# Flat step lists for the filling and draining of a two-layer transformer's second attention

## The chip, the cores and the metric

The kernel runs on one core of a Trainium2 chip. Its time is the device time of one execution in microseconds (us). A core has five engines with queues of their own: TensorE (matmuls into PSUM; PE in the profile, its weight loads PEld), VectorE (DVE), ScalarE (ACT), GpSimd (POOL) and SyncE (SP), which here issues the transfers. Each runs its queue in order and waits on semaphores. PSUM has eight banks of 128 x 512 floats.

## What is computed

Two transformer layers with layer norm after each sublayer, on x of 2 x 512 x 256 in float32:

```python
x = layernorm(x + L0_attn(x))   # 16 heads of 16; relu(scores + 0.1), causal, divided by the row's sum
x = layernorm(x + L0_ffn(x))    # Hadamard transforms, silu(gate) * up, inner width 1024
x = layernorm(x + L1_attn(x))   # 32 query heads, 8 key heads of 64; rms norm, rope, window of 64, softmax
x = layernorm(x + L1_ffn(x))    # silu(gate) * up, inner width 1024
```

## The kernel before

Most products are made in three matmuls of high and low parts (`three`, L380): each operand is kept as a rounded high part, written by ScalarE, and a low part, the difference, written by VectorE (or by GpSimd for weights, L1200). So each result that feeds a further product costs a ScalarE and a VectorE instruction beside the matmuls.

Every engine has a program of its own that walks through the same list of steps and executes those that concern it. The first part, attention of layer 0, is a list for each engine (`TENSOR_FIRST` and so on). Behind it stands one common list, `LATER` (L140 to L179), of large steps:

- `ffn(layer, n)`, n from 0 to 15 (batch n // 8, block of 128 inner rows n % 8): the up of block n (12 matmuls of 512 columns), then the down of block n - 2 (12 of 256 columns). ScalarE makes silu and the high part, VectorE the product and the low part. The hidden rows have three buffers.
- `attn1(k)`, 22 passes for the 16 groups of layer 1's attention (batch k // 8, key head k % 8). A pass runs, in an order written out for each engine (`TENSOR_PASS` and the others, L46 to L54), the pieces of several groups: `proj1` of group k - 1 (four of 1), transposes of normed rows `turn1k`, `turn1q` and `scores1` of group k - 4, transposes of probabilities `turn_p` and `pv1` of group k - 5, `out1` of group k - 6. VectorE makes cosines, sums, `normed`, `maxima`, `probs`; ScalarE squares, copies, `exps`; GpSimd sines and inverse root mean squares.
- `ln(layer, b)`: addition to the rows, statistics, and (after GpSimd's inverse deviation) normalisation of all four row blocks of a batch, in one piece; `xt(layer, b)`: their transposes.
- `chunk(name, c)`: the split of a chunk of weights. SyncE loads chunks in the order of `CHUNKS` into three slots; each load waits for the split of the chunk three before.

`LATER` starts `attn1` 0, 1 and 2 behind `ffn(0, 13)`, `(0, 14)` and `(0, 15)`, then runs whole passes; `ffn(1, 0)` and `(1, 1)` stand behind passes 19 and 20, the other steps of the second network behind the last pass. `xt(3, 1)` stands behind `ffn(1, 2)`. `ln_last` (L994) takes the last layer norm by halves.

Results go to six PSUM banks in turn (`claim`, L367); banks 6 and 7 are the accumulators `y` of the downs and of `out1`. A claim waits until the bank's last user has read it. Buffers of layer 1 lie over those of layer 0: `roped`, `q_t`, `k_t`, `probs` over layer 0's network weights, `ug1` and `down1` over the weights `qkv`. `normed(0)` (L1093) therefore waits for the last down of layer 0.

## Time and profile before

| | us |
|---|---|
| median of three runs (lowest, highest) | 527.74 (526.45, 528.85) |
| the profiled execution | 527.04 |
| its span, first to last instruction | 524.4 |
| mean granted clock of TensorE | 0.979 |

The stages of the profiled execution: attention of layer 0 until about 100 us; layer 0's network from 100 to 180.8; layer 1's attention from 165 to 451.9, of which the six passes 7 to 12 take 234.24 to 325.04; the second network from 451.9 to 517.1; the last layer norm and the store until 524.4. Busy times are those of the hardware profiler; a matmul's time on the timeline overlaps with the next one's, so start-to-start differences give its rate. The number in brackets behind a timeline row is the idle time ahead of it and who ended it.

### The profile page before, as it was taken

To read this page: it belongs to the slowest core of one execution; us is meant where nothing else is said; L and a number is where in the kernel's file an instruction comes from. 1 tells how busy PE (TensorE), PEld (TensorE's weight loads), DVE (VectorE), ACT (ScalarE), POOL (GpSimd) and SP (SyncE) were. 2 spreads that over 40 slices of the span, in tenths; PEclk is the share of its full clock that TensorE was granted. 3 is DMA by queue.
4 is the path that set the end of the run, shared out by engine and by line. 5 is a ranking of instruction groups with operands and counts; after the bars stand their busy time and mean duration, and the time that the engine had idled before them with its cause. 6 is when DMAs were issued, how large, how long until landed. Compare 5 with 4: busy or idle time off the path is not lost.

```text
span 524.4 us, 10779 instructions
## 1 busy us (share of the span) xinstructions
PE 472.9 (90%) x3848; PEld 400.3 (76%) x3848; DVE 385.0 (73%) x675; ACT 335.9 (64%) x940; POOL 236.1 (45%) x167
## 2 busy tenths in 40 slices
PE   2899997999999975999999999988996988899994
PEld 2454654788889964899999999978896877788884
DVE  4455597778562689998898998889889974543534
ACT  3555555634643439888888989859888798332230
POOL 0377537221640756655566566545656523400001
PEclk9999998999999997999999999989999899999998
DMA  8500010033310000000000000001001222000101
GB/s 272 176 16 2 2 41 0 1 120 92 97 66 20 1 1 0 23 20 3 22 23 21 21 23 21 8 15 40 24 12 50 62 62 81 1 0 1 41 0 40
DMA packets 8611, 19.96 MB, mean 38 GB/s; under 512 B 1392, under 2 KB 2928, under 8 KB 8432
## 3 DMA queue, kind: packets, MB, share of 16 engines
q1 hardware_dynamic: 8560, 19.29, 11.9%
q8 instruction: 31, 0.51, 0.4%
q14 instruction: 20, 0.16, 0.1%
HBM read 18.23 MB, written 1.05 MB: 37 GB/s over the span
## 4 chain that ended last, share of the span: by engine, by line
PE 72%; DVE 11%; ACT 8%; issue 5%; POOL 1%; DMA 1%; DVEq 0%; POOLq 0%; ACTq 0%; SPq 0%
PE psum L383 16%; PE psum L385 15%; PE psum L384 15%; PE psum L614 5%; PE psum L430 4%; PE psum L602 4%; PE psum L592 4%; ACT probs L846 4%; PE psum L448 4%; PE psum L573 2%; DVE minus_max L1122 1%; PE psum L582 1%; DVE rope_cos_part L1078 1%; DMA raw_chunks<-in_w 1%; DVE out_t_low L897 1%
## 5 line engine op out<-in xcount | busy, mean ns | idle before, releaser
L846 ACT ACTIVATE probs<-psum,minus_max 128x128 f32<-128x128 f32 x256 | 92.6, 398 | 18.7 <-PE psum L592 10.4
L1240 POOL TENSOR_TENSOR rope_sin_part<-qkv_rows,sin_weighted 128x640 f32<-128x640 f32 x32 | 49.1, 1556 | 62.3 <-DVE rope_cos_part L1091 39.5
L1249 POOL TENSOR_TENSOR rms_inverse<-rms_inverse,minus_half 128x20 f32<-128x20 f32 x16 | 64.0, 3999 | 1.3
L846 ACT ACTIVATION_READ_ACCUMULATOR probs<-psum,minus_max 128x1 f32 x256 | 60.4, 236 | 0.0
L818 ACT CAST hidden_high<-hidden 128x512 fp32r<-128x512 f32 x32 | 19.8, 620 | 62.4 <-DVE hidden L1037 62.4
L1122 DVE TENSOR_REDUCE minus_max<-psum 128x4 f32<-128x512 f32 x64 | 42.4, 684 | 15.7 <-PE psum L592 14.3
L383 PE MATMUL psum<-x_t_high,ug_high 128*128 128x512 f32 x128 | 51.2, 400 | 0.0
L385 PE MATMUL psum<-x_t_high,ug_low 128*128 128x512 f32 x128 | 50.7, 396 | 0.0
L384 PE MATMUL psum<-x_t_low,ug_high 128*128 128x512 f32 x128 | 50.4, 394 | 0.0
L1116 DVE TENSOR_TENSOR probs<-probs,prob_inverse 128x512 f32<-128x512 f32 x64 | 47.6, 744 | 2.2
L383 PE MATMUL psum<-qkv_high,x_t_high 128*128 128x384 f32 x128 | 46.3, 362 | 0.0
L823 ACT COPY qkv_rows<-psum 128x384 f32<-128x384 f32 x64 | 32.4, 509 | 19.0 <-PE psum L385 19.0
L1200 POOL TENSOR_TENSOR wout_low<-raw_chunks,wout_high 128x512 fp32r<-128x512 f32 x16 | 20.8, 1301 | 52.2 <-ACT wout_high L751 52.2
L385 PE MATMUL psum<-qkv_high,x_t_low 128*128 128x384 f32 x128 | 43.6, 341 | 0.0
L384 PE MATMUL psum<-qkv_low,x_t_high 128*128 128x384 f32 x128 | 43.6, 341 | 0.0
L614 PE MATMUL psum<-probs_t,v_rows 128*64 128x128 f32 x512 | 35.7, 282 | 8.7 <-ACT probs_t L854 8.7
L936 DVE TENSOR_SCALAR weights_t<-psum 128x384 f32<-128x384 f32 (+1 forms) x48 | 26.6, 596 | 21.3 <-PE psum L430 21.3
L383 PE MATMUL psum<-wout_high,out_t_high 128*128 128x256 f32 x128 | 38.7, 302 | 2.5 <-DVE x_rows L962 2.5
L775 ACT ACTIVATE weights_t<-psum,bias_threshold 128x384 f32<-128x384 f32 (+1 forms) x48 | 27.0, 616 | 21.7 <-PE psum L430 21.7
L1207 POOL TENSOR_SCALAR_AFFINE_SELECT weights_t<-weights_t 128x512 f32<-128x512 f32 x32 | 21.8, 694 | 36.8 <-DVE weights_t L936 21.0
L1040 DVE TENSOR_TENSOR hidden_low<-hidden,hidden_high 128x512 fp32r<-128x512 f32 x32 | 22.2, 692 | 22.0 <-ACT hidden_high L818 22.0
L614 PEld LDWEIGHTS psum<-probs_t,v_rows 128*64 128x64 f32 x512 | 28.0, 138 | 13.1 <-issue 8.5
(146 smaller groups left out, 1403.4 us busy)
## 6 DMA issues: line engine op xcount, KB each, us to landing
raw_chunks<-in_ug SPq DMA_DIRECT2D x8, 512.0 KB, 3.9
raw_chunks<-in_wout SPq DMA_DIRECT2D x16, 256.0 KB, 2.8
raw_chunks<-in_qkv SPq DMA_DIRECT2D x8, 384.0 KB, 3.3
raw_chunks<-in_x SPq DMA_DIRECT2D x2, 512.0 KB, 4.5
raw_chunks<-in_w SPq DMA_DIRECT2D x2, 512.0 KB, 6.4
down_tree<-in_down SPq DMA_DIRECT2D x1, 1024.0 KB, 8.4
x_rows<-in_x_rows SPq DMA_DIRECT2D x2, 512.0 KB, 4.8
raw_chunks<-in_down SPq DMA_DIRECT2D x2, 512.0 KB, 3.4
```

The lines of the kernel that those rows point to most:

```text
L383: nc.tensor.matmul(o, ah_, bh_, start=first, stop=False, **kw)
L384: nc.tensor.matmul(o, ah_, bl_, start=False, stop=False, **kw)
L385: return nc.tensor.matmul(o, al_, bh_, start=False, stop=last, **kw)
L614: mm = nc.tensor.matmul(o[64 * h2:64 * h2 + 64, cols], v1[:, k % 5, 1 - q4 % 2, 2 * half_ + q4 // 2, :], prt[:, 2 * half_ + h2, cols], sta ...
L775: nc.scalar.activation(wt[:, hg % 2, h4, at:at + w], o[:, 0:w], ACT.Relu, bias=bias0[:]).then_inc(done, 1)
L823: nc.scalar.copy(qraw[:, k % 2, t, :], o[:, 0:GV]).then_inc(done, 1)
L846: e = nc.scalar.activation(pr[:, c, q, :], o[:, q * P:(q + 1) * P], ACT.Exp, bias=negm[:, c, q:q + 1], accum_out=psum1[:, c, q:q + 1])
L936: nc.vector.tensor_scalar(wt[:, hg % 2, h4, at:at + w], o[:, 0:w], -ATTN_THRESHOLD, 0.0, ALU.add, ALU.max).then_inc(done, 1)
L1116: nc.vector.tensor_tensor(pr[:, c], pr[:, c], pinv[:, c, :].rearrange("p (q a) -> p q a", a=1).to_broadcast([P, 4, P]), ALU.mult).then_inc ...
L1122: nc.vector.tensor_reduce(negm[:, c, :], o.rearrange("p (q w) -> p q w", q=4), AX.X, ALU.max, negate=True).then_inc(mx_done[c], 1)
L1240: last = nc.gpsimd.tensor_tensor(ov[:, :, :, z, :], rv[:, :, :, 1 - z, :], sv[:, :, :, z, :], ALU.mult)
L1249: nc.gpsimd.tensor_tensor(r, r, half[:], ALU.pow).then_inc(rr_done, 1)
```

## The change

`LATER` is replaced by five parts. `BETWEEN` holds ups 4 to 9 and downs 2 to 7 of layer 0 with the chunks of `qkv` 0 to 5 and `ln(1, 0)`. Then a list for each engine (`TENSOR_FILL` and so on) holds the rest of layer 0's network, passes 0 to 6 in single pieces, `ln(1, 1)` in pieces and both transposes. `STEADY_STEPS` are passes 7 to 12 as before. A second list for each engine (`TENSOR_DRAIN` and so on) holds passes 13 to 21 in single pieces, ups 0 to 7 and downs 0 to 5 of layer 1, `ln(2, 0)` and `ln(2, 1)` in pieces. `LAST` holds the rest, the last three downs by halves of the rows. `ffn` is split into `up` and `down`. The high and low parts of weights lie side by side for each chunk, so that layer 1's buffers can take their places piece by piece, with waits for the pieces' last readers; layer 1's hidden rows have six buffers. The pieces of a pass inside the four lists may stand in another order than in `TENSOR_PASS` and the others.

```diff
-EARLY_AT = [NI + 5, NI + 6, NI + 7]
+STEADY = (7, 13)
 SLOTS = 3
-FLAG = 2
+HIDDEN_SLOTS = [3, 6]
-FFN1_CHUNKS = [("ug1", c) for c in range(4)] + [("down1", c) for c in range(2)]
+FFN1_CHUNKS = [("ug1", 0), ("ug1", 1), ("down1", 0), ("ug1", 2), ("ug1", 3), ("down1", 1)]
+FFN1_OVER = [(8 * i + 7) // 6 for i in range(len(FFN1_CHUNKS))]
+TENSOR_FILL = [("up", 0, 10), ("down", 0, 8), ("down", 0, 9), ("up", 0, 11), ("xt", 2, 0), ("down", 0, 10),
+    ("up", 0, 12), ("up", 0, 13), ("proj1", 0, 0), ("proj1", 0, 1), ("down", 0, 11), ("proj1", 0, 2), ("proj1", 0, 3),
+    ("up", 0, 14), ("down", 0, 12), ("up", 0, 15), ("down", 0, 13), ("proj1", 1, 2), ("down", 0, 14), ("down", 0, 15),
+    ("proj1", 1, 0), ("proj1", 1, 1), ("proj1", 1, 3), ("proj1", 2, 2), ("proj1", 2, 3), ("proj1", 2, 0),
+    ("proj1", 2, 1), ("xt", 2, 1), ("turn1q", 0, 1), ("turn1k", 0), ("turn1q", 0, 0), ("proj1", 3, 1),
+    ("scores1", 0, 0), ("proj1", 3, 0), ("proj1", 3, 2), ("proj1", 3, 3), ("scores1", 0, 1), ("turn1q", 1, 0),
...
+VECTOR_FILL = [("up", 0, 10), ("up", 0, 11), ("up", 0, 12), ("xt", 2, 0), ("up", 0, 13), ("up", 0, 14),
+    ("values1", 0), ("up", 0, 15), ("square_sums", 0), ("cosines", 0), ("ln_add", 1, 1, 0), ("ln_stats", 1, 1, 0),
+    ("ln_add", 1, 1, 1), ("ln_stats", 1, 1, 1), ("rope_sums", 0), ("ln_norm", 1, 1, 0), ("ln_norm", 1, 1, 1),
+    ("square_sums", 1), ("values1", 1), ("normed", 0), ("values1", 2), ("cosines", 1), ("xt", 2, 1),
...
+TENSOR_DRAIN = [("out1", 7, 0), ("proj1", 12, 1), ("turn1q", 9, 0), ("turn1k", 9), ("turn_p", 8, 1), ("proj1", 12, 0),
...
+    ("out1", 13, 0), ("turn_p", 14, 2), ("turn1q", 15, 1), ("turn_p", 14, 0), ("turn_p", 14, 1), ("scores1", 15, 0),
+    ("turn_p", 14, 3), ("scores1", 15, 1), ("pv1", 14, 0), ("out1", 13, 1), ("pv1", 14, 1), ("up", 1, 0),
+    ("out1", 14, 0), ("turn_p", 15, 0), ("turn_p", 15, 1), ("turn_p", 15, 2), ("turn_p", 15, 3), ("out1", 14, 1),
+    ("pv1", 15, 0), ("pv1", 15, 1), ("up", 1, 1), ("out1", 15, 0), ("out1", 15, 1), ("up", 1, 2), ("down", 1, 0),
+    ("up", 1, 3), ("up", 1, 4), ("down", 1, 1), ("up", 1, 5), ("up", 1, 6), ("down", 1, 2), ("down", 1, 3),
+    ("down", 1, 4), ("xt", 3, 1), ("up", 1, 7), ("down", 1, 5)]
+VECTOR_DRAIN = [("values1", 11), ("rope_sums", 10), ("probs", 8, 3), ("maxima", 9, 0), ("maxima", 9, 1),
+    ("square_sums", 11), ("normed", 10), ("pv1", 8, 0), ("maxima", 9, 3), ("maxima", 9, 2), ("probs", 9, 0),
+    ("probs", 9, 1), ("ln_add", 2, 0, 0), ("pv1", 8, 1), ("ln_stats", 2, 0, 0), ("ln_add", 2, 0, 1), ("cosines", 11),
+    ("probs", 9, 2), ("ln_stats", 2, 0, 1), ("probs", 9, 3), ("values1", 12), ("ln_norm", 2, 0, 0),
...
+def last_steps():
+
+    s = []
+    for n in range(8, B * NI):
+        s.append(("up", 1, n))
+        if n != 12:
+            s.append(("down", 1, n - 2 if n < 12 else n - 3))
         if n == NI + 1:
             s.append(("ln", 3, 0))
-    s.append(("ln_last",))
+    for half_ in range(2):
+        s += [("down", 1, n, half_) for n in range(B * NI - 3, B * NI)]
+        s += [("ln_add", 3, 1, half_), ("ln_stats", 3, 1, half_), ("ln_half", half_)]
+    s += [("ln_norm", 3, 1, half_) for half_ in range(2)]
     return s
...
         with ExitStack() as s:
             qn = place(s, "roped", [TT, GN], F32)
+            qt1 = place(s, "q_t", [2, NQ, 2, WIN], F32)
+            place(s, "until_down0", [512])
+            kt1 = place(s, "k_t", [2, T], F32)
             wol = place(s, "wout_low", [2, 2, C], F32R)
-            qt1 = place(s, "q_t", [2, NQ, 2, WIN], F32)
-            kt1 = place(s, "k_t", [2, T], F32)
             pr = place(s, "probs", [4, 4, P], F32)
...
+                if (name, c) in FFN1_CHUNKS:
+                    filled(act, ("proj1", KV + FFN1_OVER[FFN1_CHUNKS.index((name, c))], TT - 1))
...
                 o, done = take(act, ("turn1k", k))
+                if k == 0:
+                    filled(act, ("ffn", 0, NI + 6, 1))
...
                     filled(act, ("turn1p", k - 1, c))
+                else:
+                    filled(act, ("ffn", 0, B * NI - 1, 0))
...
                     filled(act, ("pv1", k - 1, c // 2))
+                else:
+                    filled(act, ("y", 1, B - 1, 1))
...
             def wout(k):
+                if k == 0:
+                    filled(act, ("y", 1, B - 1, 1))
...
                 if k == 0:
-                    filled(dve, ("y", 1, B - 1, 1))
+                    filled(dve, ("ffn", 0, NI + 3, 0))
```

## Rows read from the trace of the kernel before

**Rows 1.** The page, busy time of each engine with its share of the span.
```profile
PE 472.9 (90%) x3848; PEld 400.3 (76%) x3848; DVE 385.0 (73%) x675; ACT 335.9 (64%) x940; POOL 236.1 (45%) x167
```

**Rows 2.** Busy us by stage: stretch, length, PE, PEld, DVE, ACT, POOL, clock, DMA.
```profile
143.10:180.00 36.90, 36.62 (x217) 33.13 (x216) 19.66 (x40) 16.68 (x27) 12.76 (x9) 1.00 0.11 33
180.00:234.24 54.24, 44.04 (x377) 39.77 (x375) 49.48 (x82) 39.35 (x133) 33.56 (x21) 0.94 0.02 6
234.24:325.04 90.80, 90.80 (x866) 83.28 (x864) 82.68 (x133) 81.03 (x282) 54.90 (x31) 1.00 0.06 19
...
340.00:417.00 77.00, 68.87 (x656) 62.58 (x652) 72.01 (x115) 60.76 (x206) 44.72 (x25) 0.96 0.12 36
417.00:451.90 34.90, 29.40 (x273) 26.27 (x272) 21.00 (x36) 29.06 (x94) 11.37 (x7) 1.00 0.17 54
451.90:517.10 65.20, 63.63 (x370) 55.37 (x368) 29.49 (x58) 17.92 (x30) 4.68 (x5) 1.00 0.03 9
```

**Rows 3.** Timeline of TensorE: start, us, instruction, idle time ahead and its end.
```profile
201.90 0.90 PE L573 MATMUL psum<-identity,roped 128*128 128x128 f32 x3 [6.09 <-DVE roped L1107]
...
344.24 0.38 PE L383 MATMUL psum<-wout_high,out_t_high 128*128 128x256 f32 x1 [2.53 <-DVE x_rows L962]
...
406.48 0.33 PE L614 MATMUL psum<-probs_t,v_rows 128*64 128x128 f32 x2 [2.67 <-ACT probs_t L854]
...
457.59 0.33 PE L487 MATMUL psum<-identity,x_rows 128*128 128x128 f32 x1 [1.32 <-DVE x_rows L978]
```

**Rows 4.** Busy us in two short stretches of the drain, columns as above.
```profile
345.10:348.50 3.40, 3.40 (x16) 3.30 (x16) 1.78 (x8) 0.13 (x1) 1.27 (x2) 0.53 0.00 0
407.00:410.40 3.40, 3.40 (x24) 3.07 (x21) 3.33 (x7) 3.40 (x18) 3.23 (x3) 0.54 0.48 143
```

**Rows 5.** VectorE's waits from 174.5 to 234.3: total us, times, longest.
```profile
DVE x_rows L978 <- POOL ln_rstd L1220: 1.5, 1, 1.5
...
DVE square_sums L1084 <- POOL rms_inverse L1249: 0.9, 1, 0.9
```

**Rows 6.** Timeline of TensorE behind the last down of layer 0: first and last of 24.
```profile
180.80 0.34 PE L383 MATMUL psum<-qkv_high,x_t_high 128*128 128x384 f32 x1
...
184.86 0.34 PE L385 MATMUL psum<-qkv_high,x_t_low 128*128 128x384 f32 x1
```

**Rows 7.** Timelines of VectorE and TensorE at the end of pass 6.
```profile
229.95 1.22 DVE L1107 TENSOR_TENSOR roped<-rope_cos_part,rms_inverse 128x1024 f32<-128x1024 f32 x1
...
234.24 0.33 PE L573 MATMUL psum<-identity,roped 128*128 128x128 f32 x1
```

**Rows 8.** Drain: timelines, VectorE's waits of 325 to 452, groups of the page.
```profile
348.46 1.39 DVE L978 TENSOR_SCALAR x_rows<-x_rows,ln_mean_var,ln_rstd 128x256 f32<-128x256 f32 x4 [1.55 <-POOL ln_rstd L1220]
...
DVE minus_max L1122 <- PE psum L592: 6.8, 5, 2.6
...
396.37 2.50 POOL L1200 TENSOR_TENSOR ug_low<-raw_chunks,ug_high 128x1024 fp32r<-128x1024 f32 x1
396.59 2.44 DVE L1067 COPY v_rows<-qkv_rows 128x256 f32<-128x256 f32 x1
412.49 2.06 DVE L1116 TENSOR_TENSOR probs<-probs,prob_inverse 128x512 f32<-128x512 f32 x1
420.80 1.70 DVE L1116 TENSOR_TENSOR probs<-probs,prob_inverse 128x512 f32<-128x512 f32 x1
...
L1116 DVE TENSOR_TENSOR probs<-probs,prob_inverse 128x512 f32<-128x512 f32 x64 | 47.6, 744 | 2.2
L1200 POOL TENSOR_TENSOR wout_low<-raw_chunks,wout_high 128x512 fp32r<-128x512 f32 x16 | 20.8, 1301 | 52.2 <-ACT wout_high L751 52.2
```

**Rows 9.** Timelines of TensorE and VectorE at the end.
```profile
516.78 0.28 PE L385 MATMUL psum<-down_high,hidden_low 128*128 128x256 f32 x1
...
516.38 0.69 DVE L962 TENSOR_TENSOR x_rows<-psum,x_rows 128x512 f32<-128x512 f32 x1 [1.53 <-PE psum L385]
...
518.06 0.66 DVE L962 TENSOR_TENSOR x_rows<-psum,x_rows 128x512 f32<-128x512 f32 x1
```

More of the change, by code:

```diff
@@ L387, in _, with first @@
             acc = {}
+            begun = set()
+            def first(step, k):
+                new = (step, k) not in begun
+                begun.add((step, k))
+                return new
             def x_ready(layer, b):
@@ new lines, in up @@
+            def up(layer, n):
+                b, i = divmod(n, NI)
+                if i == 0:
+                    x_ready(1 + 2 * layer, b)
+                if layer == 0:
+                    emptied(pe, *[("prep_ug", i // 2, m) for m in range(KB)])
+                else:
+                    chunk_wait(pe, ("ug1", i // 2))
+                wh, wl = [up_weights(layer, i // 2, z) for z in range(2)]
+                for u in (1, 0):
+                    o, done = claim(("ffn", layer, n, u))
+                    for kb in range(KB):
+                        at = kb * 512 + (i % 2) * 256 + u * P
+                        mm = three(o, (wh[:, at:at + P], wl[:, at:at + P]), (xh[:, b, kb, :], xl[:, b, kb, :]),
+                                   kb == 0, kb == KB - 1)
+                    mm.then_inc(done, 1)
@@ L959, in ln_add @@
             def ln_add(layer, b, half_):
+                if layer == 0 and half_ == 0:
+                    dve.wait_ge(rows_in[b], 16)
                 o, done = take(dve, ("y", layer, b, half_))
```

297 lines of the change are left out of this document (157 added, 140 removed), and 41 rows, old and new, of tables (SCALAR_DRAIN, SCALAR_FILL, SCALAR_FIRST, TENSOR_DRAIN).

## The prediction

> **What bounds the kernel now.** I read the busy shares first. TensorE is busy for 472.9 of 524.4 us, and no other engine is above 385.0 [rows 1]. That share is an average, so I cut the span into stages [rows 2]. In the steady passes of layer 1's attention (234.24 to 325.04, six passes of 15.13 us) TensorE is busy for all of 90.80 us, VectorE for 82.7 and ScalarE for 81.0: TensorE sets the pace and VectorE has 1.35 us to spare in a pass. The losses lie at both sides of that stretch. While the pipeline fills (143.1 to 234.24), TensorE stands for 0.3 + 10.2 us. While it drains (340 to 451.9) it stands for 8.1 + 5.5 us, and in the second feed-forward network for 1.6 us, of which 1.3 are one stall [rows 3].
>
> Next I asked who is full where TensorE stands. From 180 to 234.24 VectorE is busy for 49.5 of 54.2 us, and from 340 to 417 for 72.0 of 77.0 us [rows 2]. So there TensorE waits for a vector engine that has hardly any room: 91% and 94% busy against 91% in the steady stretch. From 417 to 451.9 nobody is full (TensorE 29.4, ScalarE 29.1, VectorE 21.0 of 34.9 us): that is a chain of short steps. In two of the stalls the granted clock fell from 2.4 to 1.2 GHz afterwards while TensorE had work: both stretches of 3.4 us show a mean near one half [rows 4], so each cost about 1.7 us.
>
> This gives floors. If all idle time of TensorE and both slow stretches went, the fill could give 10.5 us and the drain 13.6 + 3.4 = 17.0 us. VectorE's floor is lower: it has the same work as before, so by it the fill gives only its own idle time there, and the drain up to 417 only 5.0 us.
>
> **The change, part by part.** The sets of instructions are the same in both kernels; nothing is computed more or less. What changes is their order in each engine's queue.
>
> *Fill.* Before, the queues run whole feed-forward steps (an up and the down two behind), then whole passes. The new lists interleave: the first projections stand ahead of ups 14 and 15, passes are mixed with the last downs, and layer norm comes in pieces. The new places of the buffers allow it: the normed rows no longer wait for the last down of layer 0 but for up 11. This wait doesn't bind before, since the last down ends at 180.80 [rows 6], ahead of the first normed rows; I cost it at nothing. Three of the eight projection steps that stood ahead of the last down now stand behind it. One projection step is (184.86 + 0.18 - 180.80) / 4 = 1.06 us [rows 6], so the last down ends 3.2 us earlier, at 177.6.
>
> What does VectorE make of that? Its waits in the fill are, first, 1.5 us for the layer norm's inverse deviation and 0.9 us for the inverse root mean square [rows 5]. Layer norm in pieces puts the sum of the rotated rows between statistics and normalisation, so the first wait goes; the earlier projections take the second. That is 2.4 us, and it is what VectorE gains by the end of the fill. TensorE can gain more, as far as VectorE's results are ready early. The last normed rows of the fill end at 229.95 + 1.22 = 231.17, and their first transpose starts at 234.24 [rows 7]: 3.1 us to spare. So TensorE can gain up to 2.4 + 3.1 = 5.5 us, and the steady passes, in which VectorE has 1.35 us to spare each, let it make up the lost lead. The stall of 6.1 us ahead of the second pass's transposes [rows 3] shrinks, since now four projections and both score steps stand between the first and second normed rows. Ahead of the first normed rows a stall grows: with three projections moved behind the last down TensorE is out of work at 186, while VectorE has the layer norm and two sums to do first, until 189 or 190. I count 4.5 us for the fill, nearer to 5.5 than to 2.4 because TensorE, not VectorE, sets the passes that follow; both ends stay in the range, and at the low end a gain of only 1 us, should the new stall cost more.
>
> *Added waits.* Layer 1's buffers now overlap layer 0's in smaller pieces, so ScalarE gets waits of its own: the first keys' copy for up 14, the first exponentials for up 15, the first copy of probabilities and the first output weights for the last down, each chunk of the second network's weights for one projection group of the second half. Behind each the whole of ScalarE's queue waits. By TensorE's order the awaited step ends before the producer of the waiting one begins (the last down at 177.6, the first probabilities after 199; the projections four and more passes ahead of the chunks), so they cost nothing; if TensorE's order didn't cover them, each would cost at most one up, 2.9 us.
>
> *Drain.* Layer norm of the first half of the batch was queued whole at the end of pass 13. TensorE stood 2.53 us before it could start the next accumulation [rows 3], then had a slow stretch [rows 4], and VectorE itself stood 1.55 us for GpSimd [rows 8]. Now its first addition stands ahead of the last product of pass 8 and the cosines, probabilities and values of the next passes stand between its pieces. This removes 1.55 us from VectorE; of the other 3.5 us that it idles up to 417, mostly waits for scores (6.8 us in all, with those behind 417) [rows 8], I take 2. Together 3.5 us. From 417 on the step chain decides: scores of the last pass, maxima, exponentials, transposes, product, output. The new lists turn the keys and queries of passes 14 and 15 ahead of earlier output products, so that the last scores come sooner, and put output products and the first up of layer 1's network where TensorE waits for exponentials. The last pass's own chain through ScalarE and VectorE stays: its exponentials, its four copies, its two products. Of the 5.5 us that TensorE idles there [rows 2] I take 3, and so the last output product ends at 451.9 - 3.5 - 3 = 445.4. The first stall of the drain goes; the second [rows 3] shrinks. Below these values nothing but 1.5 us for the layer norm is sure; above them stands 13 us, if VectorE's 5.0 us and most of what TensorE loses behind 417 and to the clock come back. Those are the ends for the drain.
>
> *Start of the second network.* The transposes of the second half wait 1.32 us for layer norm [rows 3], after one up and one down. The new list has five ups and five downs in between, with six instead of three buffers for the hidden rows: 1.3 us off, and nothing is late next, since the weights of the fourth chunk are loaded and split long before the up that reads them. The queue of loads keeps its order except that down chunk 0 moves ahead of the third up chunk; the whole core moves 36 to 54 GB/s there [rows 2], so nothing for it.
>
> *End.* The last accumulation ends at 517.1 on TensorE [rows 9]. Its addition starts only at 518.06, because VectorE is still at the first half, which began at 516.38. With the last three downs by halves the first half is complete three half-steps earlier, and the second addition starts with the last matmul: 518.06 - 517.1 = 1.0 us. The final normalisation's wait for GpSimd stays. The same number of matmuls runs, so the halving costs nothing on TensorE.
>
> Sum: 4.5 + 6.5 + 1.3 + 1.0 = 13.3 us. The profiled execution took 527.04 us (span 524.4), which gives 513.7; the median of the three runs is 0.7 us higher, so 514.4 us.
>
> **A rule weighed.** VectorE's copy of values at 396.59 took 2.44 us, where GpSimd ran a subtraction of 2.50 us from 396.37, and two products of probabilities took 2.06 and 1.70 us where their mean is 0.744 us [rows 8]. So a collision can hold VectorE for nearly the whole of GpSimd's instruction; these three cost about 2 + 1.3 + 1.0 = 4.3 us, and they are in the sum as they stand. The Trainium skill (SBUF — State Buffer, Who interferes with whom) says that VectorE instructions with two SBUF inputs, and some copies, contend with GpSimd instructions that read SBUF, and that the loser blocks for the whole instruction. By that rule, the trace agrees. It speaks against a list that fills VectorE's gaps, since a fuller VectorE meets more of GpSimd's instructions; by the rows alone the sum stays at 13.3 us, by the rule at its worst it is that of the last rival.
>
> **The rivals.** *VectorE is the bound (15 in 100).* Then TensorE gets nothing beyond VectorE's own idle time in the fill and little in the chain: 2.4 + 3.5 + 1.3 + 0.5 = 7.7, so 520.0. For it: 91 and 94% busy where it matters. Against it: the lead of 3.1 us, and steady passes in which it recovers.
>
> *Near TensorE's floor (10 in 100).* Fill 8, drain 13, 1.3 and 1.0: 23.3 us, so 504.4. For it: no engine's work forbids it behind 417. Against it: VectorE's floor before that.
>
> *No change (7 in 100).* The stalls only move: the new wait at 186 and others like it in the drain take the place of 6.1, 2.5 and 2.7 us; only start and end give, 2.3 us, so 525.4.
>
> *Slower by collisions (6 in 100).* In the packed drain each of GpSimd's two-input subtractions hits VectorE: eight of 1.3 us for the output weights and five of 2.5 us for the second network's chunks [rows 8], 22.9 us in all, where 4.3 us are lost already. The other 18.6 us against the 13.3 won give 5.3 us more than before: 533.0. It decides from 13.3 us of added blocking. Against it: the same subtractions beside a VectorE that is 94% busy cost only 4.3 us now.
>
> **How the numbers follow.** The forecast has 62 in 100; most of its spread is 509 to 519. The range of 506 to 522 takes in the first rival; it leaves out the floor, no change and the slower case, and they hold 23 in 100, less the part of the floor case that reaches above 506, so about 20. A measurement of this kernel can tell 0.5% from no change (525.1 to 530.4). Faster by more: 62 + 15 + 10 = 87; same 7; slower 6.
>
> **What would show it.** Steps right: no TensorE wait for the normed rows near 200 above 2 us, one of 2 to 4 us near 186 to 190; steady passes of 15.13 us that begin about 4.5 us earlier; no wait for the layer norm's addition at pass 14; the last output product ending 10 to 12 us earlier; the transposes of the second half without a wait; 6.2 instead of 7.3 us from the last matmul to the end. It is wrong if VectorE's busy time in the drain grows by over 5 us (collisions), if steady passes lengthen, or if the granted clock falls in new places while TensorE has work.

## The result and the profile after

The changed kernel took 519.73 us (median of four runs, 518.33 to 521.9) against 527.1 us for the kernel before (526.25 to 528.85): ratio 0.986, 95% interval 0.9815 to 0.9899. Timed again later in five rounds it took 520.17 us against 528.34 us, ratio 0.9845 (0.982 to 0.987). The forecast was 514.4 us with a range of 506 to 522. So the sign and the range held. Of the forecast gain of 13.3 us, 7.4 to 8.2 us came.

The profiled execution took 520.81 us with a span of 519.1 us. Busy times hardly differ from [rows 1]: no work went away, it stands closer together.

```profile
PE 475.5 (92%) x3848; PEld 399.3 (77%) x3848; DVE 384.5 (74%) x675; ACT 335.8 (65%) x940; POOL 240.5 (46%) x167
```

The stages again, cut where they now end: fill, steady passes, drain in two parts, second network, tail (stretch, length, busy us of PE, PEld, DVE, ACT, POOL, granted clock, DMA). They answer [rows 2].

```profile
181.00:235.00 54.00, 47.04 (x379) 42.40 (x379) 48.39 (x81) 42.15 (x139) 35.52 (x20) 0.94 0.02 6
235.00:326.00 91.00, 91.00 (x872) 83.37 (x866) 82.90 (x136) 81.11 (x282) 55.69 (x32) 1.00 0.07 19
...
341.00:417.00 76.00, 67.17 (x651) 59.74 (x648) 71.56 (x116) 62.44 (x215) 47.38 (x27) 1.00 0.14 42
417.00:449.10 32.10, 30.86 (x287) 26.71 (x286) 19.51 (x38) 27.34 (x88) 7.62 (x4) 1.00 0.14 45
449.10:512.70 63.60, 63.38 (x369) 55.28 (x367) 32.22 (x62) 18.50 (x31) 7.69 (x7) 1.00 0.03 9
512.70:519.10 6.40, 0.00 (x1) 0.00 (x0) 3.05 (x9) 0.00 (x0) 1.73 (x3) 0.69 0.24 82
```

Behind 417 TensorE stands for 1.2 us where it stood for 5.5. Ahead of it, it still stands for 8.8 of 76 us, and VectorE is as full as it was. Next, TensorE's timeline, where it still waits (start, us, instruction, idle time ahead and its end). The stalls of 6.09, 2.53 and 1.32 us of [rows 3] are gone, and others stand elsewhere.

```profile
191.25 1.12 PE L696 MATMUL psum<-identity,roped 128*128 128x128 f32 x4 [2.92 <-DVE roped L1238]
...
201.72 0.39 PE L705 MATMUL psum<-window_mask,eye_twice 64*128 64x512 bf16 x2 [1.04 <-ACT probs L977]
204.26 1.04 PE L696 MATMUL psum<-identity,roped 128*128 128x128 f32 x5 [1.25 <-ACT probs L977]
...
406.17 0.65 PE L688 MATMUL psum<-identity,roped 128*128 128x128 f32 x4 [0.96 <-DVE roped L1238]
407.68 0.63 PE L696 MATMUL psum<-identity,roped 128*128 128x128 f32 x4 [0.85 <-DVE out_t_low L1033]
413.25 0.39 PE L705 MATMUL psum<-window_mask,eye_twice 64*128 64x512 bf16 x2 [2.20 <-issue]
```

To compare many kernels I cut TensorE's timeline at four events that all of them have: A is the end of the last product with the Hadamard matrix (it prepares layer 0's last chunk of up weights, 1.6 us behind the second down), B the end of group 10's second projection (it lies in pass 11, one of the steady passes), C the end of the last output product, D the last matmul. A to B is what the expectations below call the part from the second neuron's product to the start of pass 10. Where they and I speak of a piece "of pass k", such as the scores of pass 14, the piece of group k is meant. "Half speed" is the time in that part during which the granted clock was 0.5 (1.2 GHz).

| kernel | median us | A | A to B (half speed) | B to C (half speed) | C to D | D to span's end |
|---|---|---|---|---|---|---|
| before | 527.1 to 528.3 | 116.39 | 183.91 (6.8) | 151.75 (3.4 + 3.4) | 65.02 | 7.3 |
| changed | 519.73 | 117.75 | 183.57 (3.4 + 3.4) | 147.85 (0) | 63.54 | 6.4 |
| again | 520.17 | 116.52 | 182.50 (0) | 147.76 (0) | 63.54 | 6.4 |
| fill_old | 520.39 | 116.74 | 183.90 (6.8) | 149.31 (3.4) | 63.54 | 6.4 |
| drain_old | 525.76 | 118.65 | 182.55 (3.4) | 152.80 (3 x 3.4) | 65.02 | 6.4 |
| last_whole | 521.65 | 117.40 | 183.71 (3.4 + 3.4) | 147.81 (0) | 63.54 | 7.3 |
| no_low | 518.74 | 116.69 | 184.55 (6.8) | 145.92 (0) | 63.54 | 6.4 |
| fill2 | 519.63 | 117.15 | 182.10 (6.8) | 149.26 (3.4) | 63.54 | 6.3 |
| warm | 521.17 | 116.69 | 184.88 (3.4) | 149.22 (3.4) | 63.54 | 6.4 |
| drain_old_warm | 524.87 | 116.73 | 183.84 (3.4) | 151.75 (3.4) | 65.01 | 6.4 |
| ln_pool | 522.73 | 116.42 | 184.63 (6.8) | 149.63 (3.4) | 63.54 | 6.4 |
| late_ug | 517.65 | 117.21 | 183.56 (3.4 + 3.4) | 146.51 (0) | 63.54 | 6.4 |
| best | 520.29 | 116.81 | 184.82 (6.8) | 146.88 (0) | 63.54 | 6.4 |
| fill3 | 523.04 | 116.97 | 187.63 (6.8 + 6.8) | 147.78 (3.4) | 63.55 | 6.4 |

The parts up to A hold the same work in all of them: A differs with a half-speed stretch of 3.4 or 6.8 us near 86 us. Two executions of one kernel differ by up to 3.6 us, and the time goes with the clock: the changed kernel's spans of 516.6 and 516.9 us had mean granted clocks of 0.989 and 0.990, those of 519.1 and 520.2 us 0.983. So the parts say more than a single total. The kernel before, timed beside each group of variants, had medians of 527.0 to 528.3 us, so between groups a difference of medians of about 1 us says little by itself.

From before to changed the parts add up: 0.3 to 1.4 us in A to B, 3.9 to 4.0 in B to C, 1.5 in C to D, 0.9 behind D, and 0.6 outside the span (see below), 7.2 to 8.4 us in all.

### The profile page after: what moved, and what is told of

Its sections match the earlier page's. It is cut to its first block, busy times and chain, and to the rows that moved or that the text cites. A ratio compares the mean times of both kernels' runs of the same rounds, so it can differ in the third digit from the quotient of the medians.

```text
span 519.1 us, 10798 instructions
## 1 busy us (share of the span) xinstructions
PE 475.5 (92%) x3848; PEld 399.3 (77%) x3848; DVE 384.5 (74%) x675; ACT 335.8 (65%) x940; POOL 240.5 (46%) x167
## 3 DMA queue, kind: packets, MB, share of 16 engines
HBM read 18.23 MB, written 1.05 MB: 37 GB/s over the span
## 4 chain that ended last, share of the span: by engine, by line
PE 77%; DVE 11%; ACT 5%; issue 4%; DMA 1%; POOL 0%; DVEq 0%; POOLq 0%; SPq 0%; ACTq 0%
PE psum L499 17%; PE psum L501 16%; PE psum L500 15%; PE psum L553 5%; PE psum L725 4%; PE psum L715 4%; PE psum L737 4%; PE psum L571 4%; PE psum L696 3%; ACT probs L977 3%; DVE minus_max L1253 2%; PE psum L705 2%; DVE roped L1238 1%; DVE square_sums L1215 1%; DMA raw_chunks<-in_w 1%
## 5 line engine op out<-in xcount | busy, mean ns | idle before, releaser
L1372 POOL TENSOR_TENSOR rope_sin_part<-qkv_rows,sin_weighted 128x640 f32<-128x640 f32 x32 | 51.2, 1623 | 48.6 <-DVE rope_cos_part L1222 42.3
L499 PE MATMUL psum<-x_t_high,ug_high_low 128*128 128x512 f32 x128 | 51.1, 399 | 0.0
L501 PE MATMUL psum<-x_t_high,ug_high_low 128*128 128x512 f32 x128 | 50.7, 396 | 0.0
L500 PE MATMUL psum<-x_t_low,ug_high_low 128*128 128x512 f32 x128 | 50.5, 395 | 0.0
L499 PE MATMUL psum<-qkv_high_low,x_t_high 128*128 128x384 f32 x128 | 47.1, 368 | 3.1 <-ACT qkv_rows L950 1.7
L500 PE MATMUL psum<-qkv_high_low,x_t_high 128*128 128x384 f32 x128 | 43.5, 340 | 0.0
L501 PE MATMUL psum<-qkv_high_low,x_t_low 128*128 128x384 f32 x128 | 43.4, 339 | 0.0
L987 ACT COPY probs_t<-psum 128x512 f32<-128x512 f32 x64 | 37.4, 626 | 0.5 <-PE psum L725 0.3
L725 PE MATMUL psum<-identity,probs 128*128 128x128 f32 x256 | 36.2, 275 | 1.4 <-ACT probs L977 1.2
L499 PE MATMUL psum<-down_high_low,hidden_high 128*128 128x256 f32 x128 | 36.4, 284 | 0.5 <-issue 0.5
```

The costliest lines, as they stand in the source:

```text
L499: nc.tensor.matmul(o, ah_, bh_, start=first, stop=False, **kw)
L500: nc.tensor.matmul(o, ah_, bl_, start=False, stop=False, **kw)
L501: return nc.tensor.matmul(o, al_, bh_, start=False, stop=last, **kw)
L725: mm = nc.tensor.transpose(o[:, q * P:(q + 1) * P], pr[:, c, q, :], ident[:])
L987: nc.scalar.copy(prt[:, c, :], o).then_inc(done, 1)
L1372: last = nc.gpsimd.tensor_tensor(ov[:, :, :, z, :], rv[:, :, :, 1 - z, :], sv[:, :, :, z, :], ALU.mult)
```

## The experiments

**Once more, unaltered.**

> The changed kernel itself once more, unaltered, beside the three that follow and timed in the same rounds as they are: 519.7 us by its first four runs (518.3 to 521.9), and with it the yardstick for the others. Nothing else is asked of it than how far its half-speed stretches move from one execution to the next: spans of 516.6 to 520.2 went with mean granted clocks of 0.990 to 0.983.

Its part A to B is 1.1 us shorter than in the first profile of the same kernel and holds no half-speed stretch; B to C agrees within 0.1 us. So the gain of 3.9 to 4.0 us in the drain repeats, and by these two the fill's is between 0.3 and 1.4 us.

**The fill's lists undone.** TENSOR_FILL and its three siblings hold the order of before:

```
...
+TENSOR_FILL = SCALAR_FILL = VECTOR_FILL = GPSIMD_FILL = fill_old()
```

> The changed kernel with layer 1's passes 0 to 6 and the rest of layer 0's network put back into the pass-by-pass order of before; buffers, the drain and the split tail stay as changed. Theory (the profile of the changed kernel gained only 0.3 us in the fill against its own offset, because VectorE's two named waits only moved): 519.5 to 521, that is 0 to 1 us above the changed kernel, and pass 7 starts about 234.7 us after the same half-speed stretches. Rival A (the prediction's sum: the lists of the fill are worth 4.5 us and the one profiled run hid it behind two extra half-speed stretches): 524, 4.5 us above the changed kernel. Rival B (the new order of the fill costs time): 517 to 519.

Measured: 520.39 us (520.08 to 521.61), 0.2 to 0.7 us above the changed kernel, as the theory has it. Rival A falls, and so does rival B. A to B is as before to 0.01 us, stall of 6.09 us included. Over the seven kernels that have the new fill unaltered (changed, again, drain_old, last_whole, no_low, drain_old_warm, late_ug), A to B is 182.50 to 184.55, mean 183.47: the lists of the fill are worth 0.4 us, which that spread of 2 us hardly tells from nothing, though layer 0's last down ends 2.3 us earlier behind A (62.3 us against 64.6).

**The drain's lists undone.**

```
...
+TENSOR_DRAIN = SCALAR_DRAIN = VECTOR_DRAIN = GPSIMD_DRAIN = drain_old()
```

> The changed kernel with layer 1's passes 13 to 21 and the first six neurons' steps of the second network put back into the order of before; the fill and the split tail stay as changed. Theory (the drain's lists gained 3.9 us and the stall before the second network 1.5): 524.5 to 525.5, that is 5 to 5.5 us above the changed kernel, and the stalls of 2.5 and 2.7 us near 344 and 406 us, each followed by a half-speed stretch, come back. Rival A (most of the 3.9 us was the two half-speed stretches that happened to be missing in the profiled run): only 1.5 to 3 us above. Rival B (the prediction's sum): 7.8 us above, 527.5.

Measured: 525.76 us (524.9 to 527.14), ratio to before 0.997 (0.995 to 0.998). That is 5.6 to 6.0 us above the changed kernel, just over the theory's 5 to 5.5 and far from rival A's 1.5 to 3 and rival B's 7.8: the theory holds in kind. The 1.48 us between C and D come back, and the profile shows three stalls, each followed by a half-speed stretch. First TensorE's timeline, then busy times of the three stretches, whose last figures but two are the granted clock:

```profile
345.22 0.39 PE L525 MATMUL psum<-wout_high,out_t_high 128*128 128x256 f32 x1 [2.50 <-DVE x_rows L1127]
...
407.27 1.11 PE L763 MATMUL psum<-probs_t,v_rows 128*64 128x128 f32 x16 [2.63 <-ACT probs_t L1013]
...
422.01 1.97 PE L763 MATMUL psum<-probs_t,v_rows 128*64 128x128 f32 x16 [2.38 <-ACT probs_t L1013]
```

```profile
347.00:350.20 3.20, 3.20 (x13) 3.10 (x13) 1.61 (x7) 1.25 (x3) 1.27 (x2) 0.50 0.00 0
408.30:411.60 3.30, 3.30 (x18) 3.29 (x17) 3.23 (x6) 3.30 (x16) 3.22 (x2) 0.50 0.49 160
422.00:425.30 3.30, 3.29 (x23) 2.97 (x24) 3.23 (x6) 2.56 (x14) 0.79 (x1) 0.50 0.36 97
```

**The stalls filled with work.** In that kernel, two of the three stalls get products whose result is overwritten:

```
                 o, done = claim(("pv1", k, half_))
+                for _ in range({(12, 1): 11, (13, 1): 10}.get((k, half_), 0)):
+                    nc.tensor.matmul(o, eye2[:], wmask[:, 0, :], start=True, stop=True)
```

> The kernel with the drain's old order (525.76 us), with 11 and 10 extra 512-column products, overwritten right behind, in the banks of the products of probabilities and values of passes 12 and 13, ahead of TensorE's waits for the transposed probabilities (stalls of 2.6 and 2.4 us at 407.3 and 422.0 us, each followed by a half-speed stretch). Theory (part of what the old order costs is not the stall but the half clock behind it): two stretches of 3.4 us go, and 2.5 to 3.4 us with them: 522.4 to 523.3. Rival (the stalls themselves are the cost, the slow stretches lie beside waits for VectorE): within 0.7 us of 525.8.

Measured: 524.87 us (523.77 to 526.98), 0.9 us less. Neither holds. The two half-speed stretches are gone, as the theory said, and the clock is 1.00 from 400 to 452:

```profile
346.00:349.30 3.30, 3.30 (x14) 3.20 (x13) 1.68 (x7) 0.80 (x2) 1.27 (x2) 0.50 0.00 0
400.00:452.00 52.00, 47.10 (x446) 39.65 (x442) 37.94 (x57) 41.07 (x137) 22.06 (x13) 1.00 0.18 57
```

But B to C falls only from 152.80 to 151.75: two stretches cost 1.05 us, not 3.4. The extra products didn't overrun the stalls: 0.23 and 0.37 us of them are left. In the old order TensorE waits again soon after a stretch, and that wait takes up most of what the half clock cost. At the full clock TensorE meets a wait here that the kernel without the extra products doesn't have:

```profile
412.75 0.63 PE L751 MATMUL psum<-identity,probs 128*128 128x128 f32 x4 [1.09 <-DVE out_t_low L1061]
```

In the new order, where it waits less behind 413, one such stretch costs more: 149.2 to 149.6 us with it (fill_old, fill2, warm, ln_pool) against 147.8 without (changed, again, last_whole), 1.4 to 1.8 us. All seven have the stall of 2.2 us, so it alone doesn't decide whether the stretch comes.

**The last downs whole again.**

```
-        s += [("down", 1, n, half_) for n in range(B * NI - 3, B * NI)]
+    s += [("down", 1, n) for n in range(B * NI - 3, B * NI)]   # once, ahead of both halves
```

> The changed kernel with the last three second projections of the network done as whole 512-column products again instead of by halves; all else as changed. Theory (the first half's addition and transfer now lie beside the second half's products): 520.5 to 520.9, 0.8 to 1.1 us above the changed kernel, and the time from the last product to the span's end is back from 6.4 to 7.3 us. Rival (the six half-width products cost as much as the hidden addition gives back, each half paying its own start): the same time within 0.3 us.

Measured: 521.65 us (521.03 to 522.14), 1.5 to 1.9 us above the changed kernel, 7.3 us from the last matmul to the end. C to D is 63.54 in both: the halving costs TensorE nothing. (The products have 256 columns in both kernels, since the halves are of the rows: the expectation's "512-column" and "half-width" products are a slip.) The parts give 0.9 us for the tail, as the theory says; the median lies 0.8 us above the theory's range, which is within the scatter. VectorE's timeline of this kernel (last matmul until 512.45) and of the changed one (until 512.70) shows the mechanism, the answer to [rows 9]: the addition of the first half has moved beside TensorE's last products.

```profile
511.77 0.69 DVE L1101 TENSOR_TENSOR x_rows<-psum,x_rows 128x512 f32<-128x512 f32 x1 [2.97 <-PE psum L501]
...
513.45 0.66 DVE L1101 TENSOR_TENSOR x_rows<-psum,x_rows 128x512 f32<-128x512 f32 x1
```

```profile
510.58 0.69 DVE L1101 TENSOR_TENSOR x_rows<-psum,x_rows 128x512 f32<-128x512 f32 x1 [1.53 <-PE psum L501]
...
512.74 0.69 DVE L1101 TENSOR_TENSOR x_rows<-psum,x_rows 128x512 f32<-128x512 f32 x1 [0.39 <-PE psum L501]
```

**GpSimd's subtractions in the drain left out.**

```
+                if name in ("ug1", "down1"):
+                    nc.gpsimd.memset(dst.bitcast(F32), 0.0).then_inc(ch_lo["pool"], 1)
+                    return
```

> The changed kernel with GpSimd's subtractions for the low parts of the second network's weights left out (a fill with zeros stands in their place, so that network lacks its low products' values but still runs all its products). It asks what GpSimd's two-input operations cost VectorE in the drain. Theory 1 (VectorE's stretched operations beside them, such as the 2.67 us product at 409.87 us, set the drain's end): 516.5 to 518, 2 to 3 us under the changed kernel, and the stall of 2.2 us at 411 us goes. Theory 2 (their cost lies beside TensorE's work, the gaps have other causes): within 0.7 us of the changed kernel, though VectorE's mean duration of the same operations falls.

Measured: 518.74 us (516.42 to 519.19), 1.0 to 1.4 us under the changed kernel; B to C falls by 1.9 us, and the stall of 2.20 us is gone. The median gained less than theory 1's 2 to 3 us and more than theory 2's 0.7 us; the part gained nearly what theory 1 asks, at no stretch of half speed in either, so here a collision does set the time. In the changed kernel it reads so, on VectorE and GpSimd:

```profile
409.87 2.67 DVE L1247 TENSOR_TENSOR probs<-probs,prob_inverse 128x512 f32<-128x512 f32 x1
412.46 0.68 DVE L1033 TENSOR_TENSOR out_t_low<-psum,out_t_high 128x512 fp32r<-128x512 f32 x1
...
409.48 2.52 POOL L1332 TENSOR_TENSOR ug_high_low<-raw_chunks,ug_high_low 128x1024 fp32r<-128x1024 f32 x1
```

The product of probabilities ends half a microsecond behind GpSimd's subtraction, and out_t_low behind it empties the bank that the scores of pass 14 wait for, the stall of 2.20 us.

**The one subtraction moved away.** Nothing is left out here; ScalarE's and GpSimd's part of one chunk go some 13 us later, from 407.9 and 409.5 to 421.3 and 422.6 us. (Not shown here: the chunk's load moves one place back in the queue of loads, and ScalarE's part of the next chunk moves behind five of its copies.)

```
-    ("exps", 13, 3), ("chunk", ("ug1", 1)), ("turn1q", 14, 1),          # ScalarE
+    ("exps", 14, 3), ("chunk", ("ug1", 1)), ("turn1k", 15),
-    ("chunk", ("ug1", 1)), ("wout", 13), ("chunk", ("down1", 0)),       # GpSimd
+    ("wout", 13), ("chunk", ("ug1", 1)), ("chunk", ("down1", 0)),
```

> The changed kernel with one preparation of the second network's weights moved back: ScalarE's rounded part from 407.9 us to about 424, GpSimd's subtraction from 409.5 us, where VectorE's multiplication of probabilities beside it took 2.67 us in place of 0.69, to about 425, where VectorE has slack. Theory (this one collision makes the stall of 2.2 us at 411 us that every kernel with the new drain shows, and in half of their runs a half-speed stretch behind it): the stall falls under 0.7 us, the drain from 147.8 to 146 us, the median from 520 to 517 to 518.3. Rival (the collision only moves to the new place): stall gone, but the drain within 0.5 us of 147.8.

Measured: 517.65 us (517.13 to 519.06), ratio to before 0.982 (0.980 to 0.984), the fastest of all. The theory holds: stall 0.22 us, B to C 146.51, no half-speed stretch. VectorE's same two instructions, GpSimd's moved one, and TensorE:

```profile
409.30 0.69 DVE L1247 TENSOR_TENSOR probs<-probs,prob_inverse 128x512 f32<-128x512 f32 x1
409.91 0.68 DVE L1033 TENSOR_TENSOR out_t_low<-psum,out_t_high 128x512 fp32r<-128x512 f32 x1
...
422.58 2.74 POOL L1332 TENSOR_TENSOR ug_high_low<-raw_chunks,ug_high_low 128x1024 fp32r<-128x1024 f32 x1 [9.46 <-ACT ug_high_low L877]
...
410.69 0.39 PE L705 MATMUL psum<-window_mask,eye_twice 64*128 64x512 bf16 x2 [0.22 <-issue]
```

Of the 2.0 us won at that stall 0.7 us are lost again behind it. So the drain gives 1.3 us. The medians differ by 2.1 to 2.5 us, but the kernel before didn't hold still between the groups either: by the ratios to it (0.9822 against 0.9845 and 0.9857, with intervals that overlap) the gain is 1.2 to 1.8 us, which agrees better with the part.

**Normed rows of pass 0 put forward.**

```
-    ("values1", 0), ("up", 0, 15), ("square_sums", 0), ...                # VectorE
+    ("values1", 0), ("square_sums", 0), ("up", 0, 15), ...
-    ("rope_sums", 0), ("ln_norm", 1, 1, 0), ("ln_norm", 1, 1, 1), ("square_sums", 1), ("values1", 1), ("normed", 0),
+    ("rope_sums", 0), ("normed", 0), ("ln_norm", 1, 1, 0), ("ln_norm", 1, 1, 1), ("square_sums", 1), ("values1", 1),
+    # TensorE and ScalarE: turn1q(0, 1), turn1k(0), turn1q(0, 0) ahead of xt(2, 1)
```

> The changed kernel with a few steps of the fill moved: VectorE sums the squares of pass 0 before the last hidden product of the network and multiplies pass 0's normed rows before it normalizes the layer norm's rows; TensorE, and ScalarE's copies with it, does the three turns of pass 0 before the transposes of the second sequence's rows. Theory (the fill gained nothing because VectorE's list puts pass 0's normed rows, which TensorE waits 2.9 us for at 188.3 us, behind a layer norm that itself waits 1.3 us for GpSimd): that stall goes to under 1 us and pass 7 starts 2 to 3 us earlier: 517 us. Rival (VectorE, busy 49.7 of 55.3 us there, is the bound of the fill, so that whatever is put forward is paid back by a later step): stall gone, but pass 7 starts within 0.7 us of where it did: 519 to 520.

Measured: 519.63 us (519.05 to 520.55), 0.1 to 0.5 us less. The stall of 2.9 us is gone, but TensorE's timeline shows it again, larger, at the scores of pass 0:

```profile
200.25 0.61 PE L705 MATMUL psum<-window_mask,eye_twice 64*128 64x512 bf16 x2 [5.58 <-ACT probs L977]
```

So something behind is full, as the rival says. Which engine, the next run asks.

**The layer norm's products on GpSimd.** Besides fill2's order:

```
+            # GpSimd, behind its inverse deviation; VectorE's ln_norm(1, 1) returns at once
+            for t in range(TT):
+                last = nc.gpsimd.tensor_scalar(xn[:, at, :], xn[:, at, :], mv[:, t, 0:1], rstd[:, t:t + 1],
+                                               ALU.subtract, ALU.mult)
```

> The kernel with the moved steps of the fill, and besides them the four normalizations of the second sequence's rows (1.39 us of VectorE, and the 1.33 us that it waited for GpSimd ahead of them) done by GpSimd itself, which stood idle for 2.98 us behind its inverses; what is computed is the same. Theory (VectorE's list is the bound of the fill): VectorE has 2.7 us less between the network's last products and pass 7, so the part from the second neurons' product to the start of pass 10 falls from 182.1 to 184.6 us (its half-speed stretches move it) to 180 to 181.5, and the median from 519.6 to 520.2 to 517.5 or below. Rival (TensorE's own work, or GpSimd's later inverses, bound the fill): the part stays at 182 or more and the median over 519.

Measured: 522.73 us (522.08 to 523.59), 2.6 to 3.0 us more than the changed kernel and 3.1 us more than fill2, its base. The theory falls. VectorE got its room and nobody gained. The tightest stretch of the fill, 186 to 205 us, as busy times in before, changed, fill2 and ln_pool:

```profile
186.00:205.00 19.00, 11.76 (x87) 10.65 (x88) 17.15 (x33) 11.02 (x40) 13.16 (x7) 0.83 0.00 0
```

```profile
186.00:205.00 19.00, 13.26 (x94) 11.86 (x93) 17.96 (x29) 11.74 (x37) 16.05 (x8) 0.90 0.00 0
```

```profile
186.00:205.00 19.00, 13.20 (x100) 12.21 (x99) 16.13 (x29) 12.29 (x39) 15.46 (x8) 0.82 0.00 0
```

```profile
186.00:205.00 19.00, 10.86 (x83) 9.67 (x82) 13.19 (x20) 10.02 (x29) 18.66 (x11) 0.83 0.00 0
```

In the last, VectorE falls to 13.2 and GpSimd rises to 18.7 of 19 us. So GpSimd, whose load the prediction never counted in the fill, has no room for this work: its inverse roots and sine products of passes 1 and 2 stand back to back behind it. The run moved the bound rather than finding it, since ln_pool's four products took 4.91 us on GpSimd, where VectorE needs 1.39:

```profile
184.53 4.91 POOL L1360 TENSOR_SCALAR x_rows<-x_rows,ln_mean_var,ln_rstd 128x256 f32<-128x256 f32 x4
189.52 0.66 POOL L1389 TENSOR_SCALAR rms_inverse<-square_sums 128x20 f32<-128x20 f32 x1
```

**Both together.**

> Both edits together: GpSimd normalizes the second sequence's rows with the fill's moved steps, and the one preparation is moved back. If each does what its theory says and they are independent: 1.5 to 2.5 us and 1.7 to 2.5 us under the changed kernel's 520.2: 515.5 to 517. If either is bound elsewhere: the better of the two alone, 517.5 to 518.5.

Measured: 520.29 us (520.17 to 520.75). The gain of the one and the loss of the other add up by the parts (184.82 and 146.88), so neither of the two outcomes came; ln_pool's theory fell in the same group of runs.

**Extra work in the fill's stalls.**

```
             def turn1q(k, hp):
-                pe.wait_ge(qn_done, k + 1)
                 o, done = claim(("turn1q", k, hp))
+                if (k, hp) in ((0, 1), (1, 0)):
+                    keep_busy(o, 12 if k == 0 else 5)
+                pe.wait_ge(qn_done, k + 1)
```

> The changed kernel with 12 and 5 extra 512-column products of the mask, overwritten right behind, in the banks of pass 0's and pass 1's first turned queries, put ahead of TensorE's wait for the normed rows (stalls of 2.9 and 1.2 us): what is computed is unchanged, TensorE only isn't idle there. Theory (the two half-speed stretches of the fill, which began at 190.9 and 204.5 us behind these stalls, follow from the idle time): they go, and 1 to 3 us with them: 517 to 518.5. Rival (the stretches come whatever TensorE does, or VectorE's pace hides them): 519.5 to 520.5, with the stretches still there or pass 7 starting as before.

Measured: 521.17 us (519.55 to 523.23), 1.0 to 1.4 us more. No stretch began near 190, but in "again" none did without the extra products either, so this says nothing on that stall. The other came, at 202.5, and the five extra products at 203.11 ran in it and took 2.32 us where they were meant to take half, so that the turns behind them started 2.0 us later behind A than in "again". Neither outcome came, and the run's six times fall in two groups, 519.6 to 519.9 us, as the changed kernel, and 522.4 to 523.2. It tells only that filling a stall can cost more than the stall.

**GpSimd's sine products first.** Base is late_ug:

```
-    ("rms_inverses", 1), ("sines", 1), ("rms_inverses", 2),             # GpSimd
+    ("sines", 1), ("rms_inverses", 1), ("rms_inverses", 2),
-    ("cosines", 1), ("xt", 2, 1), ("square_sums", 2), ("rope_sums", 1), ("maxima", 0, 0), ("normed", 1), ("maxima", 0, 1),
+    ("cosines", 1), ("maxima", 0, 0), ("maxima", 0, 1), ("square_sums", 2), ("rope_sums", 1), ("normed", 1),
+    # xt(2, 1) behind scores1(0, 1) on TensorE, behind exps(0, 1) on ScalarE, behind cosines(2) on VectorE
```

> The kernel with the one weight preparation moved back (517.65 us) and, in the fill, another order: GpSimd does pass 1's sine products before its inverse roots (at 185.2 us, where it stood idle for 3 us, in place of 191.9 us), VectorE takes the first two maxima of pass 0 before the squares of pass 2, the normed rows of pass 0 come first as in the kernel with the moved steps, and the second sequence's transposes come behind the scores of pass 0. Nothing is left out. Theory (GpSimd's order is what the fill waits for: ScalarE's copy of pass 3's first rows stands behind pass 1's sine products, which end at 195.0 us, and the exponentials, the banks and the stall of 5.6 us at 194.7 us stand behind that copy): that stall goes to under 2 us, the part from the second neuron's product to the start of pass 10 falls from 182.1 to 184.6 us to 178 to 181, and the median to 514 to 516. Rival A (VectorE's busy time, 49.7 of 55.3 us, is the bound whatever stands ahead): the part stays at 182 or more, the median within 0.7 us of 517.65. Rival B (the stall comes back at pass 1 or 2, since the inverse roots are later by 3 us): the same result as A, with a new stall of 2 us or more before pass 1's turns or pass 2's scores.

Measured: 523.04 us (521.91 to 524.45), 5.4 us above its base. The theory falls; what came is rival B and more. The stall of 5.6 us shrank only to 3.8 us, and two new ones of 2.2 us stand before the keys of pass 1 and the projections of pass 4, with two half-speed stretches of 6.8 us. One reason is plain in the rows of VectorE and GpSimd:

```profile
185.13 3.86 DVE L1120 TENSOR_SCALAR x_rows<-x_rows,ln_mean_var,ln_rstd 128x256 f32<-128x256 f32 x4
...
184.96 3.24 POOL L1372 TENSOR_TENSOR rope_sin_part<-qkv_rows,sin_weighted 128x640 f32<-128x640 f32 x2
```

VectorE's normalization took 3.86 us in place of 1.39: the sine products that I put into GpSimd's idle time fell on it, and what follows on VectorE came 2.5 us later behind A than in fill2. The run therefore doesn't settle whether GpSimd's order alone could win.

## Why the prediction was right or wrong

**Fill (4.5 us forecast, 0.4 measured): wrong.** The last down of layer 0 was to end 3.2 us earlier; behind A it ends 2.3 us earlier, since a new wait of 0.66 us stands before the first projection. The stall near 186 to 190 came as forecast (2.92 us), and so did the end of the 6.09 us one. The step that failed is "that is 2.4 us, and it is what VectorE gains". VectorE's waits between 174.5 and 235.3 us in the changed kernel, against [rows 5]:

```profile
DVE minus_max L1253 <- PE psum L715: 1.6, 3, 0.6
DVE x_rows L1120 <- POOL ln_rstd L1353: 1.3, 1, 1.3
...
DVE prob_inverse L1246 <- ACT probs L977: 1.2, 1, 1.2
```

The inverse root mean square's wait went; the layer norm's stayed. The statistics were ready at 182.97, GpSimd was at pass 0's inverse until 183.35, and then its small addition took 1.12 us. It took 0.23 us before. What held it is the very step that the new list puts between statistics and normalisation, VectorE's sum of the rotated rows. VectorE first, then GpSimd, all of the changed kernel:

```profile
182.89 1.46 DVE L1222 TENSOR_TENSOR rope_cos_part<-rope_cos_part,rope_sin_part 128x1280 f32<-128x1280 f32 x1
...
179.81 3.54 POOL L1381 TENSOR_TENSOR rms_inverse<-rms_inverse,minus_half 128x20 f32<-128x20 f32 x1
183.31 1.12 POOL L1352 TENSOR_SCALAR ln_var_eps<-ln_mean_var 128x4 f32<-128x4 f32 x1
184.52 1.05 POOL L1353 TENSOR_TENSOR ln_rstd<-ln_var_eps,minus_half 128x4 f32<-128x4 f32 x1
```

And GpSimd in the kernel before:

```profile
191.74 0.23 POOL L1219 TENSOR_SCALAR ln_var_eps<-ln_mean_var 128x4 f32<-128x4 f32 x1 [1.53 <-DVE ln_mean_var L971]
```

The addition took 1.12 or 1.38 us in all twelve profiles with the new order of these steps, and 0.23 us in before and fill_old, where no VectorE instruction stands beside it. So 0.9 of the 1.33 us are a collision that the new order made. Other waits replaced what went: VectorE is idle for 6.6 us from 174.5 to 235.3, where it was idle for 5.3 us from 174.5 to 234.3. In the 19 us from 186 VectorE is 95% busy in the changed kernel and GpSimd 84%. The other 2.1 us of the forecast, VectorE's lead at the end of pass 6, could not be used: TensorE has no wait above 0.7 us from 205 on, so its own work sets pass 7 from there, and it entered that stretch no earlier. In kind, the first rival, "VectorE is the bound", was nearer for the fill than the forecast; ln_pool shows that GpSimd is close to full there as well. Which of the two sets the fill, and what it would give with both engines' orders matched, is open: fill2, ln_pool and fill3 don't settle it.

**Added waits (costed at nothing): no sign against it, but not tested.** In ScalarE's timeline of the fill its waits stand before copies of projections, turned queries and keys, squares and scores, and none before the first probabilities' copy or the first output weights. They were not taken out one by one.

**Drain (6.5 us forecast, 3.9 to 4.0 measured, less with a half-speed stretch): half right.** From B to the scores of pass 14 it gained 1.1 us, where 3.5 were forecast; from there to the last output product 2.8, where 3 were forecast. The chain of short steps went as reasoned. VectorE's wait for the layer norm fell from 1.55 [rows 8] to 0.2 us, but the stalls around 350 to 411 us are many small ones, and the largest, 2.20 us, is a collision that I had named as a rival and priced only as a whole. The step that failed is "together 3.5 us": VectorE is idle for 4.4 of 76 us up to 417, where it was idle for 5.0 of 77 (the prediction's end at 445.4 us also leaves out the fill's 4.5 us, though the sum has them). It still waits for scores there (341 to 417, changed kernel):

```profile
DVE minus_max L1253 <- PE psum L715: 2.7, 2, 1.7
```

The collision's size was right in kind, "nearly the whole of GpSimd's instruction", and late_ug shows its worth: 1.3 us of the drain. The rule weighed there held in its kind: the loser waits for the whole instruction. The number of subtractions said little: leaving out all six of the second network's gave 1.9 us of the drain, moving a single one 1.3 us.

**Half speed (1.7 us each forecast): mis-sized in the old order.** Two stretches cost 1.05 us together there, since waits behind them take up the rest; in the new order one costs 1.4 to 1.8 us. The fill's own stretch, 6.8 us from 198.5 in the kernel before, half of it beside the stall of 6.09 us, the prediction didn't see, and it left the drain's two out of the sum, and in 6 of the 11 profiles with the new drain none came.

**Second network (1.3 us forecast, 1.48 measured) and end (1.0 forecast, 0.9 by the parts): right.** The steady passes are 15.13 us each, as before.

**What was not in the sum.** From the span to the whole time lie 2.3 us in the mean of 16 runs of before and 1.7 us in the profiled runs of most of the changed kernels, so 0.6 us more were won outside the span. All the variants have it in nearly every run (no_low's profiled one has 2.1 us), whatever was undone, so it comes with none of the three edits that were undone; the buffers' places, which all of them keep, were not tried alone.

The rival *slower by collisions* was wrong as a whole: GpSimd did not hit VectorE more often in the drain. Between B and C six VectorE instructions took over 0.25 us more than is usual for them beside a GpSimd instruction, in before and in changed alike, 6.6 us together before (the 4.3 us of the prediction are three of them) and 4.7 us in changed; in late_ug four are left, 2.1 us. *No change* is excluded by the intervals.

Of the signs named in advance, the stall near 190, the steady passes of 15.13 us, the end of the waits near 200 and for the two layer norms and 6.4 us behind the last matmul came. The last output product was to end 10 to 12 us earlier; behind A it ends 4.2 us earlier (5.4 in "again"). One sign of being wrong came as well: the granted clock fell in a new place, at 190.9, behind the new stall of 2.92 us.

## What to carry to other kernels

Before reckoning that a reordering frees a wait, look at what the other side of the wait is doing at the new time: here GpSimd, with 46% of the span busy, was 84% busy in just the 19 us that mattered. An engine's idle time beside a full neighbour is not free space either, since an instruction put there can stretch the neighbour's by most of its own length, in either direction; moving one such instruction to where the neighbour has room gave 1.3 us, a sixth of what the whole change gave. And cut the timeline at events that all variants share: single totals of one kernel differ by over 3 us here, the drain's part of it without a half-speed stretch by 0.1, though the fill's by 1.1.

## What the runs showed of the hardware

Stalls of TensorE of 2.4 to 2.7 us in the drain were each followed by a stretch of about 3.4 us at 1.2 GHz; behind the stall of 2.2 us such a stretch came in four of the seven profiles that have it. The fill's stall of 2.9 us stands in all seven profiles with the unaltered new fill, and such a stretch came right behind it in four (changed, drain_old, last_whole, late_ug) and not in three (again, no_low, drain_old_warm). So the length of a stall alone doesn't tell. Extra products in two of the stalls removed the stretches behind them. What one costs depends on what comes next: from 0.5 us where TensorE soon waits anyway to 1.4 to 1.8 us where it doesn't.

VectorE's product of 128x512 took 2.67 us beside a GpSimd subtraction of 2.52 us, and 0.69 us when that one had been moved. The other way round, GpSimd's addition on 128x4 took 1.12 us where it met VectorE's sum on 128x1280, which ran for 1.46 us, and 0.23 us without. VectorE's normalization of four blocks, which is not an operation of two tensors but of one and two columns, took 3.86 us beside GpSimd's sine products of 3.24 us and 1.39 us without. The Trainium skill (SBUF — State Buffer, Who interferes with whom) names this form among those that can take both ports and then contend with GpSimd; by that rule, the trace agrees. GpSimd needed 4.91 us for those same four blocks.
